# Moving the issue of loads, splits and two small steps in a four-stage transformer kernel on one core

## The chip, the cores and the metric

One Trainium2 chip, one core. The metric is the device time of one execution in microseconds (us). The kernel before took 3352.41 us, the median of 3 runs (3350.04 to 3352.94).

## What is computed

A residual stream x of 2048 tokens by 1024 numbers (8 x 256 x 1024) goes through two blocks, each an attention-like stage and a dense stage, all in float32:

```
x = x + tanh(g_xattn[0]) * L0_xattn(layernorm(x), ctx, ctx)     # autocorrelation
x = x + tanh(g_ffn[0])   * L0_ffn(layernorm(x), W, b, A, B, ..) # dense + gated LoRA of 4 ranks
x = x + tanh(g_xattn[1]) * L1_xattn(layernorm(x), ctx, ctx, mask, wq, wk, wv, wo)
x = x + tanh(g_ffn[1])   * L1_ffn(layernorm(x), W_base, .., enc, coefs, masks)
```

Autocorrelation works per batch and head on 256 x 128 blocks: a Fourier transform of q and k along the sequence, their product, the transform back, the top 11 lags of every column, a softmax over these, and a sum of shifted v with these weights. The second attention has 32 query heads on 8 key/value heads of 128, rotary position coding and a mask. The second dense stage is linear in its decoded update, so that update is folded into its weight first.

## The kernel before, in words

TensorE has float32 operands cut in two: `split` (L191) writes the high part h on ACT (L194) and the remainder l = source - h on DVE or POOL (L197), and `mm3` (L201) multiplies as h·h + h·l + l·h, three matmuls each. So nearly every matmul stands behind an ACT step and then a DVE or POOL step.

The kernel is written against the engines directly. `op` appends an instruction to its engine's list, `dma` (L119) to the list of the engine that issues it (SP unless said otherwise). **Each list is carried out strictly in the order in which it was written**, and an instruction whose waits are not met holds all behind it on its engine. `q.now()` is a wait on all that was issued so far; `room[...]` holds such a wait: a place in SBUF may be written again. The stages are Python generators. A driver at the end of `flamingo` (L1398 to L1452) runs them a stretch at a time, up to their next `yield`, and so settles how the lists of neighbouring stages are interleaved.

Stages, with their times on TensorE in the profile before:

- **kv** = `keys_and_values` (0 to about 400 us): wk and wv by ctx. Its last tiles are values, copied out of PSUM into `kv_oh`/`kv_ol` by a split.
- **ac** = `autocorrelation` (320 to 823 us). 16 units (two per batch of 256 tokens). It begins with loads, four `table()` splits of Fourier tables (`ac_th`/`ac_tl`), `prepare_c(0)` (split of ctx into `ac_ch`/`ac_cl`), `stats(0)` (L404, layer norm statistics of x) and `prepare_q(0)` (L417: `ac_xn`, then its split `ac_qh`/`ac_ql`). The unit loop (L621 to L680) runs three units one step apart: P1 and products (a), weights, P3, P4 (b = a-1), P5 and finish (c = a-2). The sums of products on POOL are L461/L462 (`ac_pac`) and L568 (`ac_paw`). `topk` and `weights` (L504 to L530) find the top lags in `ac_wc`, take exp (L524), sum and reciprocal (L525, L526), then the weight matrix W: DVE makes (w2 == NEG) / sum into w0 (L527), and POOL multiplies it by w1 (L529). P3 (L538) transposes W on TensorE.
- **f0** = `dense` with LoRA (805 to 1135 us). `load`, `norm`, `flip` (L709: transposes and split into `f0hh`/`f0hl`), `product` (L745), `add_bias` (L725, POOL), `leave` (L769), `gates_of` and `lora_flip` for the ranks. A side job, `second_weight` (L984), builds the folded weight of the last stage in `piece`s between f0's products: `f0raw` tiles ft (input four), wr (w1T), ut.
- **at_** = `cross_attention` (1135 to 3140 us). Four query blocks qn of 512 tokens, 32 units each (one per head): `project` (L1174 to L1178), `scores`, `turn`, `values`, `output`. In the last units of a block the next one is prepared: at w=25 `bias(qn+1)` loads the mask (`at_bi`, DVE steps L1157 to L1163), at w=27 and w=29 `norm` loads x rows into `at_xr` and normalizes them, `flip` turns them into `at_hh`/`at_hl`. at_ starts inside f0's loop (`if t == 8`).
- **f1** = `dense` again, without LoRA (3145 to 3350 us).

In `bias` and in `norm` the load and the first operation on it are written together:

```
ld = dma(f"am{s}", bi[:, s, :, :], mv[:, 4 * qn:4 * qn + 4, :], *bi_free[s], *room["end"])
z = bs[:, s, :]
a = op("vector", lambda e: e.tensor_scalar(bi[:, s, :, :], bi[:, s, :, :], 0.0, None, ALU.is_equal), ld)
```

## Time and profile before

| | before |
|---|---|
| median of 3 runs | 3352.41 us |
| the profiled execution | 3351.99 us |
| its span | 3350.2 us |
| mean granted TensorE clock | 0.971 |
| busy: PE, DVE | 3135.9 us (94%), 1996.1 us (60%) |
| busy: ACT, POOL | 1114.2 us (33%), 736.2 us (22%) |
| DMA moved | 509.50 MB, 152 GB/s |

A row of the trace gives the start in us, how long it took, engine, line, operation, output<-inputs, shape and count; in square brackets how long the engine had been idle before it and what released it. PE is the matmul side of TensorE, PEld its weight load, SPq the DMA issues of SyncE. The granted clock is the share of full speed that TensorE was given; 0.5 is 1.2 GHz and 1.0 is 2.4 GHz.

### The profile page before, as it was taken

To read this page: it belongs to the slowest core of one execution; us is meant where nothing else is said; L and a number is where in the kernel's file an instruction comes from. 1 tells how busy PE (TensorE), PEld (TensorE's weight loads), DVE (VectorE), ACT (ScalarE), POOL (GpSimd) and SP (SyncE) were. 2 spreads that over 40 slices of the span, in tenths; PEclk is the share of its full clock that TensorE was granted. 3 is DMA by queue.
4 is the path that set the end of the run, shared out by engine and by line. 5 is a ranking of instruction groups with operands and counts; after the bars stand their busy time and mean duration, and the time that the engine had idled before them with its cause. 6 is when DMAs were issued, how large, how long until landed. Compare 5 with 4: busy or idle time off the path is not lost.

```text
span 3350.2 us, 42444 instructions
## 1 busy us (share of the span) xinstructions
PE 3135.9 (94%) x15200; PEld 2614.0 (78%) x15200; DVE 1996.1 (60%) x4655; ACT 1114.2 (33%) x2314; POOL 736.2 (22%) x633
## 2 busy tenths in 40 slices
PE   8998799998898789997899999999999999999799
PEld 7887687776666678885788887788887788888687
DVE  4323388887544367775666666666666666666332
ACT  4111355553222144443333333333333333333220
POOL 2323288885312123332100000000000000000221
PEclk9999899999999899998999999999999999999899
DMA  7333212113343456765574454464545455444521
GB/s 233 126 120 132 85 47 74 45 51 110 121 173 113 157 169 224 242 239 182 176 251 164 167 173 152 157 226 151 168 147 176 151 208 165 163 164 139 194 89 62
DMA packets 232826, 509.50 MB, mean 152 GB/s; under 512 B 23170, under 2 KB 58114, under 8 KB 232618
## 3 DMA queue, kind: packets, MB, share of 16 engines
q1 hardware_dynamic: 231306, 503.46, 43.6%
q10 hardware_dynamic: 1312, 3.34, 0.3%
q8 instruction: 122, 2.00, 0.3%
q14 instruction: 86, 0.70, 0.1%
HBM read 364.13 MB, written 142.61 MB: 151 GB/s over the span
## 4 chain that ended last, share of the span: by engine, by line
PE 48%; issue 7%; DMA 5%; DVE 2%; POOL 2%; ACT 1%; SPq 1%; POOLq 0%; DVEq 0%
PE PB L209 40%; PE PB L745 5%; PE PB L1226 2%; DMA at_rawo<-in_wo 2%; POOL at_wol L197 2%; SPq L119 1%; DMA at_xr<-xd 1%; DMA at_bi<-in_mask 1%; DMA at_rawq<-in_wq 1%; PE PB L716 0%; ACT at_ss L1207 0%; DMA xd<-at_xt 0%; PE PB L1143 0%; DVE at_xt L1262 0%; DVE at_st L214 0%
## 5 line engine op out<-in xcount | busy, mean ns | idle before, releaser
L209 PE MATMUL PB<-at_woh,at_ah 128*128 128x512 f32 x1024 | 412.1, 402 | 5.8 <-POOL at_wol L197 3.4
L209 PE MATMUL PB<-at_hh,at_wqh 128*128 128x512 f32 x1024 | 402.3, 393 | 2.1 <-DMA at_wql<-wqd 2.1
L1207 ACT ACTIVATE at_ss<-at_ss,at_sm,at_bs 128x256 f32<-128x256 f32 x512 | 301.7, 590 | 305.1 <-DVE at_sm L1205 304.8
L209 PE MATMUL PB<-at_hl,at_wqh 128*128 128x512 f32 x1024 | 401.5, 392 | 0.0
L209 PE MATMUL PB<-at_woh,at_al 128*128 128x512 f32 x1024 | 400.4, 391 | 0.0
L209 PE MATMUL PB<-at_hh,at_wql 128*128 128x512 f32 x1024 | 400.1, 391 | 0.0
L209 PE MATMUL PB<-at_wol,at_ah 128*128 128x512 f32 x1024 | 399.9, 390 | 0.0
L1174 DVE TENSOR_TENSOR at_t<-PB,at_rt 128x512 f32<-128x512 f32 x128 | 88.5, 691 | 453.0 <-PE PB L209 453.0
L1262 DVE SCALAR_TENSOR_TENSOR at_xt<-PB,gt,at_xt 128x512 f32<-128x512 f32 x256 | 190.7, 747 | 119.4 <-PE PB L209 119.4
L194 ACT ACTIVATE at_ah<-PB 128x512 fp32r<-128x512 f32 x128 | 76.6, 598 | 490.1 <-PE PB L209 490.1
L209 PEld LDWEIGHTS PB<-at_woh,at_ah 128*128 128x128 f32 x1024 | 193.3, 189 | 42.9 <-POOL at_wol L197 3.8
L209 PEld LDWEIGHTS PB<-at_hh,at_wql 128*128 128x128 f32 x1024 | 193.3, 189 | 41.5
L209 PEld LDWEIGHTS PB<-at_hh,at_wqh 128*128 128x128 f32 x1024 | 194.3, 190 | 39.6 <-issue 2.3
L209 PEld LDWEIGHTS PB<-at_woh,at_al 128*128 128x128 f32 x1024 | 192.8, 188 | 41.3
L209 PEld LDWEIGHTS PB<-at_hl,at_wqh 128*128 128x128 f32 x1024 | 194.2, 190 | 35.8
L209 PEld LDWEIGHTS PB<-at_wol,at_ah 128*128 128x128 f32 x1024 | 193.6, 189 | 36.1
L217 POOL TENSOR_SCALAR at_st<-at_st 128x1 f32<-128x1 f32 x16 | 3.5, 218 | 942.9 <-DVE at_st L216 942.9
L194 ACT ACTIVATE at_pth<-PB 128x512 fp32r<-128x512 f32 x256 | 138.6, 593 | 192.8 <-PE PB L1226 192.8
L1201 DVE CUSTOM_DVE_ANT_0 at_ss<-PB,at_bi 128x256 f32<-128x256 f32 x512 | 185.7, 418 | 3.3 <-PE PB L209 3.3
L197 DVE TENSOR_TENSOR at_ptl<-PB,at_pth 128x512 fp32r<-128x512 f32 x256 | 164.1, 682 | 19.8 <-ACT at_pth L194 19.1
L209 PE MATMUL PB<-at_kh,at_qh 128*128 128x256 f32 x512 | 147.7, 288 | 15.6 <-DVE at_ql L197 15.6
L194 ACT ACTIVATE at_qh<-at_t 128x512 fp32r<-128x512 f32 x128 | 80.8, 631 | 232.3 <-DVE at_t L1178 232.3
(266 smaller groups left out, 7322.3 us busy)
## 6 DMA issues: line engine op xcount, KB each, us to landing
at_wqh<-wqd SPq DMA_DIRECT2D x96, 512.0 KB, 3.7
at_wql<-wqd SPq DMA_DIRECT2D x96, 512.0 KB, 4.6
at_woh<-wod SPq DMA_DIRECT2D x48, 1024.0 KB, 5.1
at_wol<-wod SPq DMA_DIRECT2D x48, 1024.0 KB, 8.0
at_rawq<-in_wq SPq DMA_DIRECT2D x32, 512.0 KB, 6.1
wqd<-at_wqh SPq DMA_DIRECT2D x32, 512.0 KB, 7.6
wqd<-at_wql SPq DMA_DIRECT2D x32, 512.0 KB, 8.1
at_rawo<-in_wo SPq DMA_DIRECT2D x32, 512.0 KB, 6.3
```

What stands on the lines that cost most here:

```text
L119: self.ops[eng].append((lambda e: e.dma_start(dst, src), (prior,) + waits, self.dsem[name], 16))
L194: eh = op("scalar", lambda e: e.activation(h, src, ACT.Copy), *waits)
L197: el = op(l_on, lambda e: e.tensor_tensor(l, src, asf(h), ALU.subtract), eh, *waits)
L209: e.matmul(o, a, b, start=i == 0, stop=last), *(waits if i == 0 else ()), *w, mark=last)
L217: c = op("gpsimd", lambda e: e.tensor_scalar(st[:, 14:15], st[:, 13:14], EPS, None, ALU.add), b)
L745: e["mm"] = op("tensor", lambda e_, a=a, b=b, c=c, k=k, last=last: e_.matmul(BK[bk], hidden(a, t, c), b[c][:, ns], start=c == 0 and k == 0 ...
L1174: m = [op("vector", lambda e: e.tensor_tensor(t1[:, :], BK[b], rt[:, 0, :], ALU.mult), ev, e_rt, *t_free), op("vector", lambda e: e.tensor ...
L1201: a = [op("vector", lambda e, c=c: e.tensor_tensor_reduce(out=ss[:, s, c, :], in0=PB[0][:, L * c:L * c + L], in1=bi[:, qn % 2, 2 * b + c % ...
L1207: x_of[u] = [op("scalar", lambda e, c=c: e.activation(ss[:, s, c, :], ss[:, s, c, :], ACT.Exp, bias=z[:, 4 + c:5 + c], scale=bs[:, qn % 2, ...
L1226: ev = op("tensor", lambda e, c=c, k=k: e.transpose(PB[1][:, 512 * k + P * c:512 * k + P * c + P], ss[:, s, c, P * k:P * k + P], idt[:, :] ...
L1262: f = op("vector", lambda e: e.scalar_tensor_tensor(out=xt[:, t, cs], in0=BK[6 + p % 2], scalar=gt[:, 2:3], in1=xt[:, t, cs], op0=ALU.mult ...
```

## The change

Nothing that is computed changes. The order on PE stays, but for the LoRA transposes of tiles 0 and 1, a block or two later. Its parts, from front to back:

1. **kv and ac**: `autocorrelation` yields after its loads; the driver lets value tiles' splits stand between the table, statistics and q steps; `stats(1)` and `prepare_q(2)` move from units 0 and 1's start to the end of unit 1.
2. **ac units**: W = (w2 == NEG) * w1 on DVE in one step, then times 1/sum on ACT (two tensor steps as before, the POOL one replaced by ACT's). The first split of W's sums goes from DVE to POOL. Statistics of two tiles share their POOL steps; two tiny DVE steps are added.
3. **f0**: x tiles and bias loads, norms and w splits earlier, the bT split later; flip(0) in banks 4 and 5; `second_weight`'s loads in a piece before the loop, with two `wr` buffers and two pairs of outputs.
4. **at_**: `fetch_x` and `fetch_bias` are apart from `norm` and `bias`, issued earlier: at_ starts at t == 6, bias(0) moves to t == 12; for later blocks the mask is fetched at w=21 and used at w=25, x tiles 0 and 1 fetched at w=22, used at w=27, tiles 2 and 3 fetched at w=29 and **normalized at w=30** (before: w=29).
5. **f1**: tiles 2 and 3 are loaded with 0 and 1, and normalized right after the flips of 0 and 1, ahead of `add_bias(0)`.

```
@@ weights
-                s_ = [op("vector", lambda e, k=k: e.tensor_scalar(w0[:, k, :], w2[:, k, :], NEG, tz[:, 2, k:k + 1], ALU.is_equal, ALU.mult), r[k], h)
-                      for k in V4]
-                d["W"] = tuple(op("gpsimd", lambda e, k=k: e.tensor_tensor(w1[:, k, :], w1[:, k, :], w0[:, k, :], ALU.mult), s_[k], x_[k])
+                s_ = [op("vector", lambda e, k=k: e.scalar_tensor_tensor(
+                    out=w0[:, k, :], in0=w2[:, k, :], scalar=NEG, in1=w1[:, k, :], op0=ALU.is_equal, op1=ALU.mult), r[k], x_[k]) for k in V4]
+                d["W"] = tuple(op("scalar", lambda e, k=k: e.activation(w1[:, k, :], w0[:, k, :], ACT.Copy, scale=tz[:, 2, k:k + 1]), s_[k], h)
                                for k in V4)
@@ split_W
-                    d["spW"] += split(sh[j], sl[j], pa[j], (d["sumW"][j],) + pf, l_on="vector" if j == 0 else "gpsimd")
+                    d["spW"] += split(sh[j], sl[j], pa[j], (d["sumW"][j],) + pf, l_on="gpsimd")
@@ autocorrelation, start and loop
+            yield
             table()
             prepare_c(0)
+            yield
             stats(0)
             prepare_q(0)
-            for _ in range(3):
-                table()
             yield
+            table()
+            table()
+            yield
+            table()
...
-                if a + 1 < NU:
+                if a + 1 < NU and a != 1:
                     prepare_q(a + 1)
...
+                if a == 1:
+                    stats(1)
+                    prepare_q(2)
...
-                    stats(1)
@@ dense, f1's part
-                for t in range(2):
+                for t in range(4):
                     load(t, *room["x"])
...
                 flip(1, *room["hidden"])
+                norm(2)
+                norm(3)
                 room["rest"] = yield
...
                 add_bias(1)
-                norm(2)
-                norm(3)
@@ dense, f0's part
             lora_in(0)
-            for c in range(2):
+            split_w(2, *room["rest"])
+            split_w(3, *room["rest"])
+            for c in range(C):
+                if 2 <= c < C - 2:
+                    split_w(c + 2, *room["rest"])
...
+            piece(-1)
+            norm(2)
+            norm(3)
             add_bias(0)
             add_bias(1)
-            norm(2)
-            norm(3)
@@ second_weight
-                        V["w"] = dma("wr", wr, w1T[0:P, :], *ws[1])
+                    V["w"] = [dma("wr0", wr[0], w1T[0:P, :], *ws[1]), dma("wr1", wr[1], w1T[P:2 * P, :], *ws[7])]
...
-                    if c + 1 < C:
-                        V["w"] = dma("wr", wr, w1T[P * c + P:P * c + 2 * P, :], *s)
+                    if c + 2 < C:
+                        V["w"][s] = dma(f"wr{s}", w_, w1T[P * (c + 2):P * (c + 3), :], *p_)
@@ cross_attention
+            def fetch_x(qn, t):
+                xin_of[qn, t] = dma(f"xr{t % 2}", xr[:, t % 2, :], xd[1][512 * qn + P * t:512 * qn + P * t + P, :], *xr_free[t % 2],
+                                  *stored["h"][4 * qn + t])
...
+            def fetch_bias(qn):
+                s = qn % 2
+                m_of[qn] = dma(f"am{s}", bi[:, s, :, :], mv[:, 4 * qn:4 * qn + 4, :], *bi_free[s], *room["bi"])
...
-                if n == 0:
-                    bias(0)
...
+                if more and w == 21:
+                    fetch_bias(qn + 1)
+                if more and w == 22:
+                    fetch_x(qn + 1, 0)
+                    fetch_x(qn + 1, 1)
                 if more and w == 25:
                     bias(qn + 1)
...
+                    for t in (2, 3):
+                        fetch_x(qn + 1, t)
+                if late:
                     nq.update({t: norm(qn + 1, t) for t in (2, 3)})
-                if late:
                     flip(qn + 1, 2, 0, nq[2])
@@ driver
-            if t == 8:
+            if t == 6:
                 next(at_)
```

ACT where the last value tiles of kv meet the start of ac. Before (`kv_oh` are the value tiles' high parts, `ac_th` the tables, `ac_xn` and `ac_qh` the first q):

```order
L194 ACTIVATE kv_oh<-kv_t_60 128x512 x8
...
L194 ACTIVATE ac_th<-ac_tr 128x768
L194 ACTIVATE ac_ch_73<-ac_cb 128x1024
L421 ACTIVATE ac_xn<-ac_xb_66,ac_st 128x512 x2
L194 ACTIVATE ac_qh<-ac_xn 128x1024
L194 ACTIVATE ac_th<-ac_tr 128x1024
L194 ACTIVATE ac_th<-ac_tr 128x512
L194 ACTIVATE ac_th<-ac_tr 128x1152
L194 ACTIVATE kv_oh<-PB 128x512 x4
```

And now:

```order
L194 ACTIVATE kv_oh<-kv_t_60 128x512 x8
...
L194 ACTIVATE kv_oh<-PB 128x512 x2
L194 ACTIVATE ac_th<-ac_tr 128x768
L194 ACTIVATE ac_ch_73<-ac_cb 128x1024
L423 ACTIVATE ac_xn<-ac_xb_66,ac_st 128x512 x2
L194 ACTIVATE ac_qh<-ac_xn 128x1024
L194 ACTIVATE kv_oh<-PB 128x512 x2
L194 ACTIVATE ac_th<-ac_tr 128x1024
```

Two of the four value tiles stand ahead of all that waits for ac's loads, the other two behind q.

ACT in one unit of ac, before (`ac_te` is the exp of the top lags, `ac_kk` copies for the next products, `ac_xn` and `ac_qh` the next unit's q, W is `ac_w_92`):

```order
L446 ACTIVATE ac_kk_79<-PB 1x512
L524 ACTIVATE ac_te<-ac_te 128x4x11
L478 ACTIVATE ac_kk_79<-PB 128x512 x2
L421 ACTIVATE ac_xn<-ac_xb_67,ac_st 128x512 x2
L194 ACTIVATE ac_qh<-ac_xn 128x1024
```

Now:

```order
L448 ACTIVATE ac_kk_79<-PB 1x512
L526 ACTIVATE ac_te<-ac_te 128x4x11
L531 ACTIVATE ac_w_92<-ac_w_91,ac_tz 128x256 x4
L480 ACTIVATE ac_kk_79<-PB 128x512 x2
L423 ACTIVATE ac_xn<-ac_xb_67,ac_st 128x512 x2
L194 ACTIVATE ac_qh<-ac_xn 128x1024
```

The four W steps left POOL (its L529 was just ahead of `ac_ql`) and stand on ACT ahead of the steps that make `ac_qh`.

DVE at the start of cross-attention. Before, the mask's steps stand behind the first projection (`at_t`, `at_ql`: first projection; `at_hl`: flips; `f0xt`: f0's last results):

```order
L769 SCALAR_TENSOR_TENSOR f0xt_115<-PB,gt,f0xt_115 128x512 x2
L1174 TENSOR_TENSOR at_t_175<-PB,at_rt 128x512
...
L197 TENSOR_TENSOR at_ql<-at_t_175,at_qh 128x512
L1157 TENSOR_SCALAR at_bi<-at_bi 128x1024
...
L1163 TENSOR_SCALAR at_bi<-at_bi,at_bs 128x256 x4
L1174 TENSOR_TENSOR at_t_175<-PB,at_rt 128x512
```

Now they stand far ahead of it, between flips:

```order
L214 BN_STATS at_st<-at_xr 128x6 x2
L216 BN_AGGR at_st<-at_st 128x2
L1175 TENSOR_SCALAR at_bi<-at_bi 128x1024
...
L1181 TENSOR_SCALAR at_bi<-at_bi,at_bs 128x256 x4
L197 TENSOR_TENSOR at_hl_146<-PB,at_hh_144 128x4x128
L197 TENSOR_TENSOR at_hl_147<-PB,at_hh_145 128x4x128
L847 TENSOR_TENSOR f0at<-PB,f0at 64x256
```

The statistics of x tile 3 (`at_st`) come with it, just ahead of that tile's flip.

## Rows read from the trace of the kernel before

**Rows 1.** The page, busy time, share and instructions of TensorE.
```profile
PE 3135.9 (94%) x15200; PEld 2614.0 (78%) x15200; DVE 1996.1 (60%) x4655; ACT 1114.2 (33%) x2314; POOL 736.2 (22%) x633
```

**Rows 2.** Windows: stretch, busy (count) by engine, granted clock, DMA share, GB/s.
```profile
345.40:350.80 5.40, 5.36 (x13) 4.27 (x14) 0.49 (x1) 0.00 (x0) 0.00 (x0) 0.52 0.40 147
500.74:552.44 51.70, 48.79 (x240) 40.33 (x241) 45.86 (x109) 27.95 (x50) 43.47 (x39) 1.00 0.17 61
```

**Rows 3.** Timeline, where kv meets ac.
```profile
332.86 1.29 DVE L410 BATCH_NORM_STATS2 ac_st<-ac_xb 128x6 f32<-128x512 f32 x2 [5.50 <-DMA ac_xb<-in_x]
345.44 0.77 PE L209 MATMUL PB<-kv_wvh,kv_ch 128*128 128x512 f32 x1 [19.02 <-DVE kv_ol L197]
```

**Rows 4.** Timeline, first units of ac.
```profile
404.19 1.29 DVE L410 BATCH_NORM_STATS2 ac_st<-ac_xb 128x6 f32<-128x512 f32 x2 [6.03 <-DMA ac_xb<-in_x]
409.58 0.47 PE L538 MATMUL PB<-idt,ac_w 128*128 128x128 f32 x1 [4.63 <-POOL ac_w L529]
```

**Rows 5.** Timeline, one unit of ac on POOL, ACT, DVE and PE.
```profile
521.11 1.30 POOL L197 TENSOR_TENSOR ac_slc<-ac_pac,ac_shc 128x512 fp32r<-128x512 f32 x1 [0.74 <-PE PB L553]
...
530.81 1.70 ACT L508 ACTIVATE ac_w<-ac_wc,ac_tz 128x256 f32<-128x256 f32 x4
534.54 1.05 ACT L478 ACTIVATE ac_kk<-PB 128x512 f32<-128x512 f32 x2
535.50 1.51 ACT L421 ACTIVATE ac_xn<-ac_xb,ac_st 128x512 f32<-128x512 f32 x2
536.26 2.11 DVE L527 TENSOR_SCALAR ac_w<-ac_w,ac_tz 128x256 f32<-128x256 f32 x4
536.70 2.98 POOL L529 TENSOR_TENSOR ac_w<-ac_w,ac_w 128x256 f32<-128x256 f32 x4 [2.70 <-DVE ac_w L527]
537.10 1.06 ACT L194 ACTIVATE ac_qh<-ac_xn 128x1024 fp32r<-128x1024 f32 x1
539.64 2.39 POOL L197 TENSOR_TENSOR ac_ql<-ac_xn,ac_qh 128x1024 fp32r<-128x1024 f32 x1
545.27 1.30 POOL L197 TENSOR_TENSOR ac_slc<-ac_pac,ac_shc 128x512 fp32r<-128x512 f32 x1 [0.74 <-ACT ac_shc L194]
552.44 0.47 PE L209 MATMUL PB<-ac_ch,ac_th 128*128 128x512 f32 x1 [1.71 <-POOL ac_cl L197]
```

**Rows 6.** Timeline, gaps of PE in f0.
```profile
843.20 0.76 PE L745 MATMUL PB<-f0wh,f0hh 128*128 128x512 f32 x1 [4.18 <-DVE f0wl L197]
869.41 0.45 PE L209 MATMUL PB<-f0hh,f0agh 128*68 128x256 f32 x1 [5.62 <-DVE f0raw L1011]
983.75 0.45 PE L209 MATMUL PB<-f0hh,f0agh 128*68 128x256 f32 x1 [4.55 <-DVE f0raw L1028]
1043.47 1.97 PE L1143 MATMUL PB<-idt,at_xr 128*128 128x128 f32 x8 [12.68 <-ACT at_xr L220]
```

**Rows 7.** Timeline, start of cross-attention and the ends of its query blocks.
```profile
1144.84 0.69 DVE L197 TENSOR_TENSOR at_ql<-at_t,at_qh 128x512 fp32r<-128x512 f32 x1 [0.70 <-ACT at_qh L194]
1152.79 2.65 DVE L1157 TENSOR_SCALAR at_bi<-at_bi 128x1024 f32<-128x1024 f32 x1 [7.25 <-DMA at_bi<-in_mask]
1162.87 0.55 PE L209 MATMUL PB<-at_kh,at_qh 128*128 128x256 f32 x1 [15.58 <-DVE at_ql L197]
1541.66 0.69 DVE L1157 TENSOR_SCALAR at_bi<-at_bi 128x1024 f32<-128x1024 f32 x1 [17.70 <-DMA at_bi<-in_mask]
1550.81 0.77 PE L209 MATMUL PB<-at_pth,at_vh 128*128 128x512 f32 x1 [14.97 <-DVE at_ptl L197]
1592.82 0.77 PE L209 MATMUL PB<-at_pth,at_vh 128*128 128x512 f32 x1 [10.41 <-DVE at_ptl L197]
2058.53 0.77 PE L209 MATMUL PB<-at_pth,at_vh 128*128 128x512 f32 x1 [5.28 <-DVE at_ptl L197]
```

**Rows 8.** Timeline, the norm of x tile 2 for block 2, ACT.
```profile
2124.32 1.24 ACT L220 ACTIVATE at_xr<-at_xr,at_st 128x1024 f32<-128x1024 f32 x1 [3.59 <-POOL at_st L219]
```

**Rows 9.** Timeline, start of f1.
```profile
3160.80 1.97 PE L716 MATMUL PB<-idt,f1xn 128*128 128x128 f32 x8 [10.06 <-ACT f1xn L220]
```

More of the change, by code:

```diff
@@ L707, in hidden, with flip @@
                 return x_[(t // 2) % 2][:, c, P * (t % 2):P * (t % 2) + P]
-            def flip(t, *after):
+            def flip(t, *after, b=6):
                 e, s, j = d[t], t % 2, (t // 2) % 2
@@ L866, in dense @@
                 flip(1, *room["hidden"])
+                norm(2)
+                norm(3)
                 room["rest"] = yield
                 load_bias(*room["rest"])
-                for t in range(2, NX):
+                for t in range(4, NX):
                     load(t, *room["rest"])
@@ L918, in dense @@
                 fetch_w(c, *room["w23"])
-            flip(0)
+            flip(0, b=4)
             flip(1)
@@ L933, in dense @@
                         product(t, hf, [c])
-                if c == 0:
-                    split_w(2, *room["rest"])
+                if c == 1:
                     gates_of(0)
-                    split_w(3, *room["rest"])
+                if c == 3:
+                    load_bias(*room["rest"])
+                    for t in range(4, NX):
+                        load(t, *room["rest"])
+                if c == 4:
+                    lora_flip(0)
             h = op("scalar", lambda e: e.activation(bts[:, :], btr[:, :], ACT.Copy), *e_btr)
@@ L941, in dense @@
             e_bt += [h, l, z]
-            for c in range(2, C):
-                if c + 2 < C:
-                    split_w(c + 2, *room["rest"])
-                for t in range(2):
-                    for hf in range(2):
-                        product(t, hf, [c])
-                if c == 3:
-                    lora_flip(0)
-            load_bias(*room["rest"])
-            for t in range(4, NX):
-                load(t, *room["rest"])
+            piece(-1)
+            norm(2)
+            norm(3)
             add_bias(0)
             add_bias(1)
-            norm(2)
-            norm(3)
-            piece = second_weight(raw, ws)
             for t in range(0, NT, 2):
@@ L984, in second_weight @@
         def second_weight(raw, ws):
-            ft, wr, en, ut = (raw[i][:, :] for i in range(4))
+            ft, en, ut = (raw[i][:, :] for i in (0, 2, 3))
+            wr = [raw[i][:, :] for i in (1, 7)]
+            keep = [[raw[i][:, :].bitcast(R) for i in s] for s in ((5, 6), (0, 4))]
             wsum = raw[4][:, :].rearrange("p (c n) -> p c n", c=C)
@@ L1050, in cross_attention @@
             vh, vl = ([place(f"at_{n}{i}", kb + 4 + 2 * j, [P, 4, P], R) for i, kb in enumerate((0, 144))] for j, n in enumerate(("vh", "vl")))
-            bi = place("at_bi", 8, [P, 2, 4, L])
+            bi = place("at_bi", 187, [P, 2, 4, L])
             woh, wol = place("at_woh", 32, [P, 2, 4, 512], R), place("at_wol", 112, [P, 2, 4, 512], R)
@@ L1150, in flip @@
                 hid[qn] = hid.get(qn, none) + free[b]
+            def fetch_bias(qn):
+                s = qn % 2
+                m_of[qn] = dma(f"am{s}", bi[:, s, :, :], mv[:, 4 * qn:4 * qn + 4, :], *bi_free[s], *room["bi"])
             def bias(qn):
[L1154 to L1155 removed]
+                s, ld = qn % 2, m_of[qn]
                 z = bs[:, s, :]
@@ L1316, in cross_attention @@
             flip(0, 0, 1, nq[0])
+            fetch_x(0, 2)
             room["wq", 1] = yield
             fetch_wq(1)
-            split_wq(1)
             flip(0, 1, 0, nq[1])
             flip(0, 1, 1, nq[1])
-            nq.update({t: norm(0, t) for t in (2, 3)})
-            room["kv"] = yield
+            fetch_x(0, 3)
+            nq[2] = norm(0, 2)
+            split_wq(1)
+            room["kv"] = room["bi"] = yield
             e_rt = dma("rt", rt[:, :, :], rope.rearrange("a p n -> p a n"), *room["kv"])
+            fetch_bias(0)
             load_kv(0)
-            for t in (2, 3):
-                flip(0, t, 0, nq[t])
-                flip(0, t, 1, nq[t])
+            flip(0, 2, 0, nq[2])
+            flip(0, 2, 1, nq[2])
+            nq[3] = norm(0, 3)
+            yield
+            bias(0)
+            flip(0, 3, 0, nq[3])
+            flip(0, 3, 1, nq[3])
             room["kv"] = room["end"] = yield
@@ L1407, in flamingo @@
         next(ac)
-        for _ in range(4):
-            next(kv)
+        next(kv)
+        next(kv)
         next(ac)
-        for _ in range(2):
-            next(kv)
+        next(ac)
+        next(kv)
+        next(kv)
+        next(ac)
+        next(ac)
+        next(kv)
+        next(kv)
         next(ac)
@@ L1438, in flamingo @@
                 at_.send(q.now() + stored["h"][12] + stored["h"][13])
+                next(at_)
         at_.send(q.now() + stored["h"][14] + stored["h"][15])
```

76 lines of the change are left out of this document (41 added, 35 removed).

## The prediction

> **What bounds the kernel now.** I read the page's busy times first: TensorE is busy 3135.9 of 3350.2 us [rows 1], so the time can fall only where TensorE stands still or runs at its lower clock. Then I went through TensorE's timeline for its idle times: they add up to the 214 us that these two leave, nearly all in some forty gaps of about 1 to 19 us. They lie where one stage meets the next, and at the end of each query block, not in the steady parts. Each gap's row names its releaser, and the releaser's own queue tells what it had waited for. Last, the windows: after a long gap TensorE gets a lower clock. The 5.4 us after the 19 us gap ran at 0.52 (1.2 GHz) [rows 2]. At 2.4 GHz the same work takes about half, so such a gap costs some 2.6 us more than its length; I count 2.4 where I count it.
>
> Three patterns stand behind the gaps. A load is issued right before its first use, and the in-order engine that waits for it holds back work that TensorE needs: DVE waits 17.70 us up to the mask's landing at 1541.66, and TensorE stands still for 14.97 us behind it [rows 7]. Or a buffer is alone, so that the next load starts late (the wait before 983.75 [rows 6]). Or, in the steady units of ac, POOL sets the pace: [rows 5] and below.
>
> **The terms.** The sum is made against the profiled execution, 3351.99 us (span 3350.2); the median shown, 3352.41, stands 0.4 higher, less than a measurement of this kernel can tell (about 0.2%, 7 us).
>
> *kv to ac.* TensorE waits 19.02 us for value tiles' splits [rows 3], which stand behind statistics on DVE that wait for x until 332.86. Now two tiles' splits go ahead of anything that waits for a load, and the loads are issued before them, so what follows waits little. The clock loss (2.6) goes too; I leave 2.5 us for the first q on POOL, whose step takes 2.39 [rows 5]. **-19**; if the loads still land late, -10.
>
> *Unit 1.* DVE's statistics of batch 1 wait for their load up to 404.19, and the weights behind them free TensorE at 409.58 after 4.63 us [rows 4]. They now stand behind the weights. With the clock's 2.4, less 0.5 for the q made later: **-6.5** (0 to -8).
>
> *Steady units, 14 of them.* Does the POOL step taken away help? From one `ac_slc` on POOL at 521.11 to the next at 545.27 it is 24.16 us [rows 5]. The path through it, step to step without slack: `ac_slc`, `ac_cl` and four sums on POOL; shw and wc copies on ACT; the top-k on DVE to 536.26; W on POOL 2.98; `ac_ql` 2.39 at 539.64; two sums; shc on ACT; `ac_slc`. No TensorE step is in it, and TensorE is busy 48.79 of the 51.70 us that two units take [rows 2]: **this loop, not TensorE, sets the pace**, though by little; the 1.71 us gap of every second unit [rows 5] is its trace. What does the change do to it? `ac_ql` needs `ac_qh` from ACT. Before, ACT did kk (1.05), xn (1.51) and qh (1.06) between 534.54 and 538.16, beside DVE's last top-k steps, and POOL's W hid the rest. Now four W copies stand ahead of these on ACT, and each waits for its DVE step, the first of which comes at 536.26 (four take 2.11 before; I take the same). ACT copies of this size are 1.70 for four, 0.43 each. So W ends near 538.6, kk 539.6, xn 541.1, qh 542.2, and `ac_ql` starts at 542.2 in place of 539.64: the loop grows by 2.5 us. Against this stands the merge of the statistics' POOL steps, about 0.3 a batch. 14 x 2.5 less that is **+33**. Bounds: if the loop takes the path through POOL's own work as the end, it shrinks by 2.98 at most, and TensorE's idle time, 2.91 of each 51.70, is all that is to be had: 20 over seven pairs, of which what the first and last units and W's own waits keep leaves -12. If kk's lateness holds TensorE too and its clock falls at times, +50. I take the row path, since I could follow every link. The first split of W's sums (DVE to POOL, one step of 1.30 as `ac_slc` [rows 5]) falls in POOL's idle 2.70 ahead of W: nothing. If that cover is gone it costs 1.3 a unit.
>
> *f0's start.* The 4.18 us wait for w's split (behind a DVE step that waits for bT) goes, with its clock loss; so do small waits of 1 to 2 us for gates and W; flip(0) in other banks no longer waits for the last unit's banks, though ac's own end still holds it. The 5.62 us wait for ut [rows 6] has DVE's coefficient steps ahead of it; they move two pieces earlier, and some 4 stays. **-12** (-6 to -16).
>
> *Side job.* The 4.55 us wait [rows 6] is DVE held by the w1T load in its single buffer. With two it is there: with the clock **-7** (-3 to -7).
>
> *at_ starts at t == 6.* 12.68 us is load and norm of the first x tiles [rows 6]. Both now come two tiles earlier. DVE still waits in order, so I leave about 4: **-9.5** (-5 to -13).
>
> *t == 12.* New wait: norm of tile 3 is issued just ahead of its own flip. DVE statistics 1.5, POOL 1.1, ACT 1.24 [rows 8], evictions before it: 5.7 against 1.3 before, read off this chain's like in [rows 8], and some clock: **+5.4** (0 to +8).
>
> *First scores.* 15.58 us: DVE waits for the mask to 1152.79, and the projection's steps queue behind [rows 7]. With bias gone only the second projection's chain is left, about 4.7 (the first one's ended with `at_ql` at 1144.84 + 0.69, 4.3 after its start): **-10.9** (-8 to -12). Bias itself cost 5.6 here and 3.66 at w=25; its first step took 2.65 beside a POOL step and 0.69 without one [rows 7].
>
> *Query blocks.* The mask waits of 14.97 and 5.28 [rows 7], and a third like the second, go: 14 and, with some clock, 12.8 for the two. The x wait of 10.41 [rows 7] goes: 10.5. In the first block the waits for tiles 2 and 3 shrink by 2. But norms 2 and 3 move from w=29 to w=30, right ahead of flip(2). Before, tile 2's last step ended at 2125.56 [rows 8], beside outputs of w=29; that cover is now gone: 1.5 of statistics, 1.1 on POOL and two steps of 1.24 stand open, some 5 us, part of it behind the last weight products. +2 in each of the two later blocks. **-35** (-25 to -40).
>
> *f1.* 10.06 us [rows 9]: norms 2 and 3 wait for loads and stand behind two POOL bias steps of 2.3. Both gone: **-11.9** (-8 to -12).
>
> Sum: -19 - 6.5 + 33 - 12 - 7 - 9.5 + 5.4 - 10.9 - 35 - 11.9 = -73.4. 3351.99 - 73.4 = 3278.6, so **3279 us**.
>
> **A rule beside it.** The Trainium skill says (SBUF — State Buffer, section "SBUF: two separate sides") that DVE and GpSimd share a port pair as an exclusive lock: a DVE step with two SBUF inputs and a GpSimd step that reads SBUF block each other for a whole instruction. The pair 2.65 and 0.69 above agrees. The mechanism as this kernel's rows have it is the third rival.
>
> **Rivals.**
>
> (a) *The unit loop doesn't grow*, since W copies fit into ACT's idle time or POOL's relief wins. For it: POOL is busy 43.47 of 51.70 [rows 2], of which W is two steps of 2.98. Against it: POOL is idle for 2.70 right before W, so its load isn't the limit, the order is. Steady units then give -12 in place of +33: 3279 - 45 = **3234**.
>
> (b) *Loads land late anyway.* Issued earlier, they stand behind other loads on SP and share the transfer engines with weight traffic; the mask and x waits shorten by half only. Half of kv to ac, blocks and f0's end (19 + 35 + 9.5 + 10.9) is 37, some kept: **3310**. Against it: the mask has four units (58 us) of lead now.
>
> (c) *DVE's new W step collides with POOL.* It has two SBUF inputs where the old one had one. Each unit it can be held by one POOL step of 1.3 [rows 5], and the split moved to POOL lengthens POOL's stretch just there. 14 x 1.3 = 18, with some more clock loss: **3299**.
>
> (d) *Slower: TensorE loses its clock through ac.* A longer loop leaves TensorE idle 4 us a unit. If that gathers in one gap a unit, the clock falls in each, as after the gap of 19.02 [rows 2, 3]. TensorE takes 24.4 us a unit at full clock (half of 48.79), and the other terms (-106) are used up when each of 14 units takes 7.6 us more than its 25.85 of now, 33.4: that is at a share at 1.2 GHz of 0.37. At 0.45 it is 35.4, 9.5 more: +133, less 106, **3379**. Against it: the longest steady gap is 1.71 [rows 5], and half-clock work inside idle time costs nothing until TensorE is the limit.
>
> (e) *The change isn't what it says.* Its orders shown above are what is said, so this has no chance of its own.
>
> **Chances.** Forecast 0.52; (a) 0.22; (b) 0.11; (c) 0.10; (d) 0.04; 0.01 for no change. The forecast's own range, from the terms' ends (not all at once), is 3262 to 3297. The full range takes in (a) with some room and (c), and most of (b): 3222 to 3308. Faster by over 0.2%: all but (d) and the last, 0.95.
>
> **What would show it.** In the changed profile: no gap over 4 us of TensorE at 320 to 350, and none behind `at_bi`; the DVE row of the mask without a DMA wait; two units in 56 us or more in place of 51.7, with `ac_ql` waiting for `ac_qh` (not for DVE); a gap of some 5 us before flip(2) of each later block and at t == 12. I am wrong on the main term if the units of ac take 51.7 or less, and on the rest if the mask and x rows still end their waits on DMA.

## The result and the profile after

The changed kernel takes **3321.67 us**, the median of 4 runs (3316.34 to 3328.27), against 3352.68 (4 runs, 3350.04 to 3353.28) before: 0.991 of it, 95% interval 0.9891 to 0.9929. It is faster by 31 us; 73 had been forecast, and 3321.67 lies above the range given (3222 to 3308).

The page after, busy times (beside [rows 1]) and the granted TensorE clock in 40 slices, in tenths:

```profile
PE 3134.4 (94%) x15200; PEld 2612.5 (79%) x15200; DVE 1989.6 (60%) x4655; ACT 1140.3 (34%) x2378; POOL 692.2 (21%) x553
PEclk9999999999999989999999999999999999999999
```

TensorE's work is the same, 3134.4 against 3135.9 us. So of the 29.5 us that the span lost (3350.2 to 3320.7) 28 are idle time, 214 to 186 us. 44 us of work left POOL and 26 came to ACT. The mean granted clock is 0.977, against 0.971 before.

Where did it go? The instructions on TensorE are nearly the same in both traces, so a stage's gain can be read from the start of one and the same matmul in both. The last column is that offset (after minus before) at the end of a stretch, "measured" is its change across the stretch, and a minus is a gain:

| stretch | forecast | measured | offset at its end |
|---|---|---|---|
| kv to ac | -19 | -18.9 | -18.9 |
| unit 1 of ac | -6.5 | 0 | -19.0 |
| steady units | +33 | +48 | +29 |
| ac's end and f0's start | -12 | -7 | +22 |
| side job in f0 | -7 | -2.4 | +19.6 |
| at_ started at t == 6 | -9.5 | -1.1 | +18.5 |
| t == 12 | +5.4 | +6.8 | +25.3 |
| first scores | -10.9 | -7.9 | +17.4 |
| query blocks | -35 | -35.4 | -18.1 |
| f1 | -11.9 | -11.4 | -29.5 |

So the kernel wins 84 us at seven places and gives 55 back, 48 of them in the unit loop of the autocorrelation.

The pair of units, from one `ac_slc` on POOL to the next but one, as windows (columns as in [rows 2]):

```profile
517.81:577.00 59.19, 50.68 (x242) 41.37 (x241) 46.34 (x109) 31.34 (x59) 38.00 (x29) 0.94 0.15 54
```

59.19 us in place of 51.70, though POOL has 5.5 us less to do in it. (All steady pairs agree with this one within 0.2 us.) The timeline of the unit that answers to [rows 5]:

```profile
533.65 1.40 DVE L529 SCALAR_TENSOR_TENSOR ac_w<-ac_w,ac_w 128x256 f32<-128x256 f32 x4
534.08 1.71 ACT L531 ACTIVATE ac_w<-ac_w,ac_tz 128x256 f32<-128x256 f32 x4 [2.24 <-DVE ac_w L529]
535.70 1.05 ACT L480 ACTIVATE ac_kk<-PB 128x512 f32<-128x512 f32 x2
536.65 1.51 ACT L423 ACTIVATE ac_xn<-ac_xb,ac_st 128x512 f32<-128x512 f32 x2
538.25 1.06 ACT L194 ACTIVATE ac_qh<-ac_xn 128x1024 fp32r<-128x1024 f32 x1
539.39 2.37 POOL L197 TENSOR_TENSOR ac_ql<-ac_xn,ac_qh 128x1024 fp32r<-128x1024 f32 x1 [7.88 <-ACT ac_qh L194]
545.00 1.30 POOL L197 TENSOR_TENSOR ac_slc<-ac_pac,ac_shc 128x512 fp32r<-128x512 f32 x1 [0.74 <-ACT ac_shc L194]
548.90 0.71 POOL L414 TENSOR_TENSOR ac_st<-ac_st,gt 128x2 f32<-128x2 f32 x1
549.57 2.34 POOL L197 TENSOR_TENSOR ac_cl<-ac_cb,ac_ch 128x1024 fp32r<-128x1024 f32 x1
549.64 2.29 DVE L415 TENSOR_TENSOR ac_st<-ac_st 128x2 f32<-128x2 f32 x1 [1.20 <-POOL ac_st L414]
554.66 0.77 PE L209 MATMUL PB<-ac_ch,ac_th 128*128 128x512 f32 x1 [5.12 <-DVE ac_pbw L565]
558.60 1.14 DVE L509 TENSOR_SCALAR ac_tz<-ac_t 128x4 f32<-128x4 f32 x1
```

POOL stands idle for 7.88 us and waits for ACT's `ac_qh`, which stands behind the four W steps (L531): the wait that was forecast. Two rows were not. L415 multiplies two numbers a partition, and takes 2.29 us, as long as the POOL split `ac_cl` that began 0.07 us ahead of it; DVE's products (L565), which POOL's sums and TensorE wait for, stand behind. And L509, the negation of the maxima ahead of the exp, took 0.35 us in the kernel before and takes 1.14 beside POOL's split of `ac_slw`. TensorE's gap ahead of `ac_ch` is 5.12 us in place of 1.71 [rows 5], and its matmul after it takes 0.77 in place of 0.47: the granted clock of the 2.34 us from 554.66 on is 0.50, 1.2 GHz.

Unit 1, beside [rows 4]:

```profile
395.13 0.16 DVE L415 TENSOR_TENSOR ac_st<-ac_st 128x2 f32<-128x2 f32 x1 [1.23 <-POOL ac_st L414]
395.61 1.52 ACT L423 ACTIVATE ac_xn<-ac_xb,ac_st 128x512 f32<-128x512 f32 x2 [4.97 <-DVE ac_st L416]
398.37 2.35 POOL L197 TENSOR_TENSOR ac_ql<-ac_xn,ac_qh 128x1024 fp32r<-128x1024 f32 x1 [3.27 <-ACT ac_qh L194]
400.68 2.34 POOL L197 TENSOR_TENSOR ac_cl<-ac_cb,ac_ch 128x1024 fp32r<-128x1024 f32 x1
403.12 0.77 PE L209 MATMUL PB<-ac_ch,ac_th 128*128 128x512 f32 x1 [4.91 <-issue]
```

The load is no longer waited for, but statistics, xn, q and its split now stand ahead of `ac_cl` on POOL, and TensorE waits 4.91 us for that instead of 4.63 for W: `ac_cl` ends at 403.02, TensorE goes on at 403.12. The offset had fallen from -17.3 to -26.2 where the 4.63 us wait had been; it is back at -19 shortly behind this one. L415 is in this unit as well, with no POOL step beside it, and takes 0.16 us.

f0 and the start of cross-attention, beside [rows 6] and [rows 7]:

```profile
886.13 3.61 PE L1017 MATMUL PB<-f0raw,f0raw 128*128 128x512 f32 x4 [5.22 <-DVE f0raw L1013]
946.48 2.84 PE L1017 MATMUL PB<-f0raw,f0raw 128*128 128x512 f32 x4 [2.51 <-DMA f0raw<-in_four]
1028.56 1.29 DVE L214 BATCH_NORM_STATS2 at_st<-at_xr 128x6 f32<-128x512 f32 x2 [7.00 <-DMA at_xr<-xd]
1035.06 0.36 ACT L846 ACTIVATE f0at<-PB 128x256 fp32r<-128x256 f32 x1
1036.03 2.04 PE L1035 MATMUL PB<-f0raw,f0raw 128*128 128x512 f32 x2 [12.04 <-DVE f0at L847]
1133.59 1.97 PE L1158 MATMUL PB<-idt,at_xr 128*128 128x128 f32 x8 [5.93 <-ACT at_xr L220]
1176.72 1.06 ACT L194 ACTIVATE at_wqh<-at_rawq 128x1024 fp32r<-128x1024 f32 x1 [6.60 <-DMA wqd<-at_wql]
1177.68 0.61 ACT L194 ACTIVATE at_qh<-at_t 128x512 fp32r<-128x512 f32 x1
1178.33 2.42 DVE L197 TENSOR_TENSOR at_ql<-at_t,at_qh 128x512 fp32r<-128x512 f32 x1 [3.43 <-ACT at_qh L194]
1180.90 0.55 PE L209 MATMUL PB<-at_kh,at_qh 128*128 128x256 f32 x1 [8.28 <-DVE at_ql L197]
```

The 12.68 us wait for x did not shrink, it moved: load and norm are now issued together at t == 6, DVE waits for the landing at 1028.56, and ACT's norms stand ahead of f0's own copy L846. At t == 12 the forecast wait is there (5.93). At the first scores the mask is gone, and a wq split takes part of its place: on ACT its step (`at_wqh`) waits 6.60 us ahead of the second projection's `at_qh`, and DVE's `at_ql` then takes 2.42 beside POOL's half of that split (1177.86 to 1180.20).

Query blocks and f1, beside [rows 7], [rows 8] and [rows 9]:

```profile
1585.38 0.47 PE L209 MATMUL PB<-at_pth,at_vh 128*128 128x512 f32 x1 [2.53 <-DVE at_ptl L197]
2120.33 1.97 PE L1158 MATMUL PB<-idt,at_xr 128*128 128x128 f32 x8 [6.94 <-ACT at_xr L220]
3140.26 1.22 PE L724 MATMUL PB<-idt,f1xn 128*128 128x128 f32 x8 [1.09 <-DVE f1hl L197]
```

The gaps behind the mask (14.97, 5.28) are gone, and of the one behind x (10.41) 2.53 is left. The flip of tile 2 waits 6.94 us for its norm in the last two blocks, 5.98 in the one before. f1's 10.06 is 1.09.

### The profile page after: what moved, and what is told of

It reads as the page before. It is cut to its first block, busy times and chain, and to the rows that moved or that the text cites. A ratio compares the mean times of both kernels' runs of the same rounds, so it can differ in the third digit from the quotient of the medians.

```text
span 3320.7 us, 42376 instructions
## 1 busy us (share of the span) xinstructions
PE 3134.4 (94%) x15200; PEld 2612.5 (79%) x15200; DVE 1989.6 (60%) x4655; ACT 1140.3 (34%) x2378; POOL 692.2 (21%) x553
## 4 chain that ended last, share of the span: by engine, by line
PE 62%; DVE 3%; DMA 1%; ACT 1%; issue 0%; POOL 0%; SPq 0%; DVEq 0%; ACTq 0%; POOLq 0%
PE PB L209 50%; PE PB L753 7%; PE PB L1244 3%; PE PB L724 1%; PE PB L1158 1%; DMA wqd<-at_wql 0%; ACT at_ss L1225 0%; DMA xd<-at_xt 0%; DVE at_xt L1280 0%; DVE at_ss L1219 0%; DVE at_ss L1236 0%; DVE at_ptl L197 0%; DVE at_st L214 0%; DMA at_wql<-wqd 0%; DMA f1bg<-in_b 0%
```

## The experiments

The theory: all of the lost 48 us comes from three edits inside a unit, W on ACT ahead of the next q, the new statistics and the first split on POOL. Rivals: the new order at ac's start; POOL as the limit. Four kernels take the edits back, all together and one by one. A "pair" is always the time from one `ac_slc` on POOL to the next but one.

**All three taken back.**

```
weights:  TT(w2 == NEG, 1/sum) on DVE, W multiply on gpsimd   (as before)
split_W:  l_on="vector" if j == 0 else "gpsimd"               (as before)
stats:    three POOL steps a tile                             (as before)
```

> The changed kernel with the three edits inside a unit of the autocorrelation taken back: W's multiply on POOL, the first split of W's sums on DVE, and the statistics' POOL steps one tile at a time. Theory: all that the unit loop lost, 59.2 us a pair of units against 51.7, comes from these three; the pair is 51.7 again, seven pairs give 52 us, and the time is 3270 (3264 to 3278). Rival: the loop is long because of where the first value tiles and loads now stand; then pairs stay above 57 and the time above 3300.

Measured: 3271.99 us (3270.94 to 3276.48), ratio to before 0.9763 (0.9747 to 0.9779). Its pair of units as a window:

```profile
500.06:551.77 51.71, 48.81 (x242) 40.33 (x241) 45.84 (x109) 27.98 (x51) 43.48 (x38) 1.00 0.17 62
```

51.71, as before the change. Without these three edits the change would have won 80 us. The order at ac's start has no part in the loss of the steady units. In unit 1 it has: with the three edits gone TensorE still waits 3.94 us for `ac_cl` there, in place of 4.91.

```profile
400.38 0.77 PE L209 MATMUL PB<-ac_ch,ac_th 128*128 128x512 f32 x1 [3.94 <-issue]
```

**W alone taken back.**

```
-                s_ = [op("vector", lambda e, k=k: e.scalar_tensor_tensor(... w2 == NEG) * w1 ...
-                d["W"] = tuple(op("scalar", ... w0 * 1/sum ...
+                s_ = [op("vector", lambda e, k=k: e.tensor_scalar(... w2 == NEG) * 1/sum ...
+                d["W"] = tuple(op("gpsimd", ... w1 * w0 ...
```

> Only W's multiply is back on POOL. Theory: the four W copies on ACT ahead of the next q cost the loop 2.5 to 3 us a unit; a pair falls from 59.2 to about 54 and the time to 3286 (3278 to 3296). Rival: POOL, which now also has the first split and is asked for W again, becomes the limit: the pair stays above 57, the time above 3305.

Measured: 3291.33 us (3288.54 to 3298.29), 0.982 (0.9804 to 0.9836).

```profile
509.21:563.97 54.76, 50.28 (x245) 41.96 (x244) 47.73 (x109) 28.33 (x51) 43.94 (x36) 0.97 0.16 58
```

59.2 to 54.76, so W costs 4.4 a pair, 2.2 a unit. The rival falls: POOL has its step again and the loop is shorter. 3.06 are left for the other two edits.

**Statistics alone taken back.**

```
-                c = op("gpsimd", ... z[:, :, 14:15] ...)      # both tiles at once
-                f = op("vector", lambda e: e.tensor_tensor(z[:, :, 16:17], z[:, :, 12:13], z[:, :, 15:16], ALU.mult), d)
-                f = op("vector", lambda e: e.tensor_scalar(z[:, :, 16:17], z[:, :, 16:17], -1.0, None, ALU.mult), f)
+                    c, d, f on gpsimd, for each tile
```

> Only the statistics are as before: six small POOL steps, no DVE step after them. In the changed kernel the DVE step that multiplies two numbers a partition (two SBUF inputs) took 2.29 us, as long as the POOL split beside it, and held DVE's next products. Theory: this costs the unit with statistics 1.4 us or more; the pair falls from 59.2 to 57.7 or less, seven of them give 10 us or more: 3312 (3302 to 3316). Rival: DVE's wait is covered, and the pair stays at 59.2 or grows by 0.3: 3322 to 3325.

Measured: 3309.31 us (3307.22 to 3310.32), 0.987 (0.9855 to 0.9884).

```profile
513.89:571.68 57.79, 50.53 (x242) 41.18 (x241) 43.83 (x107) 31.37 (x59) 39.17 (x32) 0.97 0.15 55
```

1.4 us a pair, 12 in all (3321.67 to 3309.31). What should have saved 0.3 a pair cost 1.4.

**First split alone taken back.**

```
-                    d["spW"] += split(..., l_on="gpsimd")
+                    d["spW"] += split(..., l_on="vector" if j == 0 else "gpsimd")
```

> Only the first split of W's sums is back on DVE. In the changed kernel a DVE step between the top-k steps (the negated maxima) took 1.14 us beside a POOL split, and 0.35 before. Theory: the split on POOL costs each unit 0.4 to 0.8 us that way, 6 to 12 us in all: 3313 (3309 to 3317). Rival: it hides in POOL's idle time ahead of the q split (7.9 us) and nothing moves: 3321.

Measured: 3312.94 us (3309.46 to 3313.61), 0.9879 (0.9864 to 0.9894).

```profile
516.10:574.31 58.21, 50.25 (x241) 41.15 (x241) 46.67 (x111) 31.17 (x59) 36.42 (x26) 0.97 0.15 55
```

The pair is 1.0 less. L509 fits: 1.14 us in every unit of the changed kernel, here about 0.36 and 1.08 by turns, so 0.8 us less a pair. POOL had room for the step (it is idle 7.88 us a unit); its neighbour on DVE had not. Together the three, taken back alone, give 4.4 + 1.4 + 1.0 = 6.8 of the 7.5 us a pair; the rest appears only when two of them are gone (with W back, 3.06 are left, of which 1.4 and 1.0 are these two).

**Why a step on two numbers takes 2.29 us.** The same arithmetic in another form:

```
-                f = op("vector", lambda e: e.tensor_tensor(z[:, :, 16:17], z[:, :, 12:13], z[:, :, 15:16], ALU.mult), d)
-                f = op("vector", lambda e: e.tensor_scalar(z[:, :, 16:17], z[:, :, 16:17], -1.0, None, ALU.mult), f)
-                e_n[b] = [(d, f)] * 2
+                e_n[b] = [(d, op("vector", lambda e, t=t: e.tensor_scalar(
+                    z[:, t, 16:17], z[:, t, 12:13], z[:, t, 15:16], -1.0, ALU.mult, ALU.mult), d)) for t in range(2)]
```

> The changed kernel with the statistics' last step (-mean times 1/std) still on DVE, but as one tensor_scalar a tile, its multiplier a scalar operand, in place of a tensor_tensor with two SBUF inputs and a tensor_scalar. Theory: the tensor_tensor was held for 2.29 us because it has two SBUF inputs while POOL runs its split; the other form is not held, takes 0.2 us, and the pair falls from 59.2 to 57.5 or so: 3310 (3305 to 3314). Rival: what holds DVE beside a POOL step does not ask how many inputs there are (the top-k's negation, a tensor_scalar, was held as well): the step still takes over 1.5 us and the pair stays at 59.

Measured: 3311.92 us (3307.53 to 3314.88), 0.9884 (0.987 to 0.9897); the pair from 514.49 to 572.05 is 57.56, 1.6 less. The step and the POOL split that begins just ahead of it:

```profile
546.23 2.35 POOL L197 TENSOR_TENSOR ac_cl<-ac_cb,ac_ch 128x1024 fp32r<-128x1024 f32 x1
546.30 0.33 DVE L415 TENSOR_SCALAR ac_st<-ac_st 128x1 f32<-128x1 f32 x2 [1.21 <-POOL ac_st L414]
```

Both tiles' steps take 0.33 us, at the same 0.07 us behind the start of `ac_cl` as the form that took 2.29. So it is not the load of DVE or the wait for POOL's result that held it. Nor is the old form slow by itself: it took 0.16 us in unit 1, with no POOL step beside it, and beside `ac_cl` (549.57 to 551.91) it ended at 551.93. What in the new form frees it isn't separated: the multiplier is a scalar operand, each tile has a step of its own, and the multiply by -1 is in it. And the count of inputs is not all of it: L509 has a single tensor input and was held as well, up to 559.74 beside a POOL step that ended at 559.71.

**The place of W on ACT, not the engine.** The four ACT steps behind the next q (xn, qh) in place of ahead of it; statistics and first split as before:

```
                 if a + 1 < NU and a != 1:
                     prepare_q(a + 1)
+                if 0 <= b < NU:
+                    weights_out(b)      # the four ACT steps, taken out of weights(b)
```

> W's last multiply stays on ACT, but is issued behind the next q (copies, normalized x and its split) instead of ahead of it; statistics and first split as before the change. Theory: not the engine but the place cost the time. The q split on POOL then waits neither for POOL's W nor for ACT's, and starts 1.4 us earlier than in the kernel before, so the loop is at most as long as before, with TensorE's own 48.8 as its floor: a pair of 50 to 51.7, time 3262 (3255 to 3270). Rival: W now comes too late for its transposes on TensorE, whose product feeds the loop through the sums: the pair is above 53, the time above 3280.

Measured: 3260.78 us (3259.75 to 3266.75), 0.9728 (0.9706 to 0.9749).

```profile
521.78:571.50 49.72, 48.67 (x241) 40.51 (x240) 44.64 (x109) 31.26 (x59) 37.64 (x30) 1.00 0.18 64
```

```profile
541.20 1.06 ACT L194 ACTIVATE ac_qh<-ac_xn 128x1024 fp32r<-128x1024 f32 x1
542.16 1.69 ACT L535 ACTIVATE ac_w<-ac_w,ac_tz 128x256 f32<-128x256 f32 x4
542.33 2.37 POOL L197 TENSOR_TENSOR ac_ql<-ac_xn,ac_qh 128x1024 fp32r<-128x1024 f32 x1 [4.24 <-ACT ac_qh L194]
...
765.88 2.53 PE L544 MATMUL PB<-idt,ac_w 128*128 128x128 f32 x8 [7.24 <-ACT ac_w L535]
```

49.72 us a pair, 2.0 below the kernel before and 1.0 above TensorE's own 48.67, so that TensorE is now all but the limit. Beside the changed kernel two other edits differ here; beside the kernel with all three taken back (3271.99, pair 51.71) only W does, and it is 11 us better. One new wait at the last unit, 7.24 us, since W there stands behind f0's first norms on ACT (L220, 762.75 to 765.43).

**The same two orders in the kernel before**, with nothing else of the change.

```
 weights(b) with (w2 == NEG) * w1 on DVE and the four 1/sum steps on ACT
 first kernel:  the ACT steps in weights(b), ahead of prepare_q(a + 1)
 second kernel: behind prepare_q(a + 1)
```

> The kernel before, with W's edit alone: the masked product on DVE, the multiply by 1/sum on ACT ahead of the next q. Taking it back from the changed kernel won 4.4 us a pair of units (59.2 to 54.8). Theory: it costs about the same alone, a pair of 55.5 to 57 in place of 51.7, and the time is slower than before by 28 to 40: 3384. Rival: alone it is harmless, since the POOL step it frees pays for it, and only with the split moved to POOL and the new statistics does it cost: a pair under 53, time within 8 of before.

> The kernel before, with the same edit, the four ACT steps behind the next q instead of ahead of it. Theory: a pair of 49.7 as in the changed kernel with this placing, 2.0 less than before; seven pairs, less some us for the last unit, where W then stands behind the dense stage's first norms: 3341 (3336 to 3346). Rival: it needs the earlier starts of the change to pay: the pair stays at 51.7 and the time at 3350 or above.

Measured: 3379.9 us (3377.39 to 3386.27), ratio 1.0088 (1.007 to 1.0106), and 3343.23 (3340.17 to 3348.05; 10 runs), ratio 0.9976 (0.9967 to 0.9985). Pairs in this order:

```profile
501.93:558.07 56.14, 50.33 (x242) 41.38 (x241) 44.42 (x109) 31.12 (x59) 37.53 (x31) 0.97 0.16 57
```

```profile
516.83:566.52 49.69, 48.62 (x242) 40.51 (x241) 44.62 (x109) 31.24 (x59) 37.65 (x30) 1.00 0.18 64
```

One edit, slower by 28 us in one place on ACT's list and faster by 9 in another (seven pairs give 14; a wait of 7.22 us at the last unit takes part of it). Between these two runs nothing but the order on ACT differs. In the order of the change it costs 4.4 us a pair here too, so neither the split on POOL nor the statistics are needed for it.

**Where the gain at t == 6 went.** Loads at t == 6, norms at t == 8:

```
             fetch_wq(0)
+            yield
             nq = {0: norm(0, 0), 1: norm(0, 1)}
...
             if t == 8:
+                next(at_)
```

> The changed kernel, with the first two x loads of the cross-attention still issued at t == 6 of the dense stage, but their norms at t == 8. In the changed kernel loads and norms were issued in one go at t == 6 and TensorE stood still for 12.04 us there, against 12.68 at t == 8 before: the wait had only moved. Theory: with a stage step of 30 us between load and norm the wait goes but for DVE and ACT queues, 3 us or less: 3312 (3308 to 3316). Rival: what was waited for is the work of the norms themselves (DVE, POOL, ACT, 4.4 us) and not the load: 6 us or more remain, 3316 to 3321.

Measured: 3315.75 us (3311.98 to 3318.29), 0.9892 (0.9873 to 0.9911). The interval overlaps that of the changed kernel (0.9891 to 0.9929), so the trace must tell: the 12.04 us gap is gone, and a new one stands at t == 8:

```profile
1056.59 1.97 PE L1158 MATMUL PB<-idt,at_xr 128*128 128x128 f32 x8 [6.94 <-ACT at_xr L220]
```

Matmuls behind it start 6.5 us earlier than in the changed kernel. So of the wait some 5 to 6 us were the load, and 7 are the norms' own chain, left open because norm and flip are issued next to each other. The theory had 3 us or less for the rest; the rival's 6 us or more is what is seen. The time lies where both ranges nearly meet and decides nothing.

**Norms of tiles 2 and 3 in unit 29 again.**

```
+                    nq.update({t: norm(qn + 1, t) for t in (2, 3)})     # in unit 29, behind fetch_x
                 if late:
-                    nq.update({t: norm(qn + 1, t) for t in (2, 3)})
```

> The changed kernel with the norms of x tiles 2 and 3 of the next query block issued in unit 29 again, right behind their loads, where it has them in unit 30. In the changed kernel the flip of tile 2 waits 6.94 us for them in blocks 2 and 3 and 5.98 in block 1; before, blocks 2 and 3 had gaps of 1.0 and 2.0 there. Theory: blocks 2 and 3 win 4 us each, block 1 nothing or a little loss, since its loads landed late before (gaps of 5.70 and 3.41): 3314 (3310 to 3318). Rival: the load wait comes back on DVE in all blocks and nothing is won: 3320 to 3324.

Measured: 3316.44 us (3309.01 to 3318.99), 0.9891 (0.9869 to 0.9913). Block 1 and block 2:

```profile
1623.95 1.29 DVE L214 BATCH_NORM_STATS2 at_st<-at_xr 128x6 f32<-128x512 f32 x2 [6.03 <-DMA at_xr<-xd]
1628.16 2.13 PE L1244 MATMUL PB<-idt,at_ss 128*128 128x128 f32 x8 [6.04 <-DVE at_ss L1236]
1633.70 0.77 PE L209 MATMUL PB<-at_woh,at_ah 128*128 128x512 f32 x1 [3.41 <-POOL at_wol L197]
...
2124.66 1.69 PE L1158 MATMUL PB<-idt,at_xr 128*128 128x128 f32 x8 [2.03 <-DVE at_hl L197]
```

By the starts of like matmuls block 1 loses 3.3 us, and blocks 2 and 3 win 2.8 and 3.3 (against 6.94 a gap of 2.03). Both sides of the theory hold: where the load is late (block 1) the move to unit 30 pays, where it is not it costs. The three together, 3 us, are less than a measurement of this kernel can tell.

**wq splits behind both projections.**

```
-                split_wq(n + 2)
+            for n in range(2):
+                split_wq(n + 2)
```

> The changed kernel with the split of the wq tiles 2 and 3 behind both projections of the first block. In the changed kernel ACT waits 6.60 us for the raw wq tile's room and load ahead of the second projection's q, and TensorE stands still for 8.28 us. Theory: the gap falls to 4.7, the length of the projection's own chain: 3.6 us, 3318 (3316 to 3320), and the profile must show it, since the times can hardly. Rival: the next stretch then waits for the later splits, and nothing is won in all.

Measured: 3321.92 us (3315.07 to 3324.58), 0.9908 (0.9887 to 0.9929), as the changed kernel.

```profile
1179.17 0.55 PE L209 MATMUL PB<-at_kh,at_qh 128*128 128x256 f32 x1 [3.82 <-DVE at_ql L197]
...
1184.48 0.76 PE L209 MATMUL PB<-at_hh,at_wqh 128*128 128x512 f32 x1 [3.68 <-POOL at_wql L197]
```

The gap falls from 8.28 to 3.82, and the next projection then waits 3.68 for the wq tile: the rival holds, nothing is won.

**All of it in one kernel.**

```
 W's ACT steps behind prepare_q (at the last unit: right behind the weights)
 statistics and first split as before
 at_: fetch_x, fetch_wq at t == 4, norms at t == 6; norm(0, 3) ahead of flip(0, 2)
 norms of tiles 2 and 3 of later blocks at the end of unit 29
```

> What the runs so far point to, in one kernel: W's last multiply on ACT behind the next q (for the last unit right after the weights, since the run with it showed a gap of 7.24 us there), statistics and first split as before the change; the first x loads of the cross-attention at t == 4 and their norms at t == 6; tile 3's norm ahead of tile 2's flip; the norms of tiles 2 and 3 of later blocks at the end of unit 29. Theory: on the 3261 of the run with W behind q, about 4 off at the last unit, 10 at the start of the cross-attention (12.2 us gap), 5 at t == 12 (5.93), 9 in blocks 2 and 3 and 3 in block 1 (gaps of 6.96 and 4.95): 3230 (3222 to 3245). Rival: the earlier norms hold DVE or ACT where f0's or unit 29's own steps need them, and half of it is lost: 3245 to 3258.

Measured: **3246.65 us** (3243.37 to 3254.63; 5 runs), 0.9694 (0.9678 to 0.9709), 104 us less than before and 75 less than the changed kernel. It missed 3230 and its range, and lies in the rival's (3245 to 3258). By the starts of like matmuls against the run with W behind q, the blocks gave 11 of 12 us and the start of at_ 7 of 10; the 4 of the last unit came to nothing, since what follows there waited on, and so did the 5 of t == 12:

```profile
1063.64 1.24 ACT L220 ACTIVATE at_xr<-at_xr,at_st 128x1024 f32<-128x1024 f32 x1 [11.69 <-POOL at_st L219]
1064.79 1.06 ACT L194 ACTIVATE at_hh<-PB 128x512 fp32r<-128x512 f32 x2
1066.23 1.94 PE L1166 MATMUL PB<-idt,at_xr 128*128 128x128 f32 x8 [6.04 <-DVE at_hl L197]
1066.72 0.69 DVE L1183 TENSOR_SCALAR at_bi<-at_bi 128x1024 f32<-128x1024 f32 x1
```

Tile 2's transposes were done by 1060.2, but their copies out of PSUM (`at_hh` on ACT, `at_hl` on DVE) now stand behind tile 3's norm: ACT waits for POOL's last statistics step, does the norm at 1063.64 and `at_hh` at 1064.79, and TensorE's transposes of tile 3 wait for `at_hl`. The mask's steps (L1183) come only after that. So the wait for the norm's chain only changed its place, 6.04 us in place of 5.93: issued ahead of tile 2's copies the chain holds these, issued behind them it holds tile 3's flip. In the later blocks tile 2's flip no longer waits for its norm, and tile 3's waits 3.07 us for `at_hl`.

## Why the prediction was wrong

Right in sign, wrong in size: -31 in place of -73. The sum had -73.4 and the trace has -29.5; the 44 us between them, by the lines of the table:

- **The steady units, 15 us.** Two steps of the sum failed here: "Against this stands the merge of the statistics' POOL steps, about 0.3 a batch", and the first split on POOL, which "falls in POOL's idle 2.70 ahead of W: nothing". Around them the mechanism was right: the loop, not TensorE, sets the pace, and ACT's four steps ahead of `ac_qh` lengthen it. W's own share was sized well, 2.2 a unit against 2.5. But the merge of the statistics costs 1.4 a batch instead of giving 0.3, because a DVE step on two numbers takes 2.29 us beside POOL's split, and the split moved to POOL costs 1.0 a batch alone: POOL did have the idle time, but the step of DVE beside it (L509) went from 0.35 to 1.14. Another 0.7 a batch shows only with two of the edits in.
- **Unit 1, 6.5 us.** "They now stand behind the weights" was right, and the load wait went. I didn't ask what `stats(1)` and `prepare_q(2)` now stand ahead of: POOL's `ac_cl`. The gap is 4.91 in place of 4.63, one unit on, and 3.94 of it stay when the three edits are taken back.
- **at_ at t == 6, 8.4 us.** "Both now come two tiles earlier. DVE still waits in order, so I leave about 4." Load and norm still go out together, so the whole wait of DVE and ACT came along, onto steps of f0 that TensorE needs: 12.04 us against 12.68. With the norms two tiles behind the loads 6.5 us come back, and a wait of 6.94 is left.
- **The side job, 4.6 us.** The w1T wait is all but gone (0.88 of 4.55) and gave 6.0 us with the clock, near the 7 of the sum. But 3.7 was lost earlier in it, most of it at a 2.51 us wait (0.52 before) for the load into the single `ft` buffer, after which the matmuls ran at the lower clock. SP issued that load right behind the reload of an x tile, which came 4.58 us behind its store in place of 2.66. No run took this part alone; why the reload came later is left open.
- **f0's start, 5 us, and the first scores, 3 us.** In f0 TensorE waits 5.22 us for the last coefficient step on DVE (L1013) and 1.88 more for ut's copy, 7.1 together where the sum left 4 and the kernel before had 5.62; and of the 4.18 us wait for w's split 1.79 are left. At the scores I took the projection's chain alone and didn't read ACT's list: the wq split ahead of `at_qh` was there before, hidden by the mask.
- **Right:** kv to ac (-18.9), t == 12 (+6.8 against +5.4), and f1 (-11.4). The query blocks (-35.4) are right as a sum and in part by luck: the three mask waits gave 32 where 27 had been put, x and tiles 2 and 3 of the first block 8 in place of 12.5, and the late norms cost 5.6 in place of 4.

Of the rivals, (a) falls: the loop did grow. (b) falls for mask and x in the later blocks: no step on DVE waits as much as 1 us for one of their loads. Two waits of DVE for a load are left, x at t == 6 (7.00 us) and the first mask (3.62 us at 1134.56, which held up nothing on TensorE). (c) had the mechanism and the wrong instruction: the Trainium skill's rule (SBUF — State Buffer, section "SBUF: two separate sides"), that a DVE step with two SBUF inputs and a GpSimd step that reads SBUF block each other for the whole instruction, is what L415 shows, 2.29 us beside POOL's split against 0.16 without one. The pair 2.65 and 0.69 that the prediction called in agreement is a step with one tensor input, like L509: it shows a hold, but not one that this rule on two inputs covers. The step that I had priced by it, W on DVE, took 1.40 us for four in place of 2.11 and met no POOL step. (d) had the right sign for the clock: it fell after each 5.12 us gap (0.50 in the 2.34 us behind it, 0.94 over the pair), but TensorE's slower work lay in idle time that the loop left anyway, and cost nothing that the pair doesn't show.
